# Neighbour maximum: word numbers added by the matrix engine, keys by five wide operations, and one joined tree over the ring slots

## What is computed

```python
def _L0_gnn_ref(X, adj):
    neg = jnp.finfo(X.dtype).min
    mask = adj != 0
    ...
        vals = jnp.max(jnp.where(mrows[:, :, None], X[None, :, :], neg), axis=1)
        has_nbr = jnp.any(mrows, axis=1)
        return (None, jnp.where(has_nbr[:, None], vals, jnp.zeros((), X.dtype)))
...
x = _layernorm(x + _L0_gnn_ref(x, adj), axis=-1)
```

## Time and profile before

| | |
|---|---|
| three plain runs, median | 4908.32 us (4907.93 to 4910.63) |
| the profiled execution, span | 5439.8 us |
| mean granted PE clock in it | 0.929 |
| PE busy | 4559.6 us (84%) |
| DVE busy | 4311.2 us (79%) |
| ACT busy | 2207.6 us (41%) |
| POOL busy | 1205.9 us (22%) |
| the neighbour maximum in the profiled execution | 0 to about 2240 us |
| in it, from 237 to 2143 us: PE, DVE, ACT, POOL busy | 1336, 1303, 900, 945 us of 1906 |

### The profile page before, as it was taken

How to read it: one execution, slowest core, us unless ns; L and a number is a source line. 1 busy time by engine, 2 the same in 40 slices (tenths; PEclk the granted TensorE clock), 3 DMA queues, 4 the chain that set the end, 5 groups by cost and what they waited for, 6 DMA issues and landing times. The chain is left out here.

```text
span 5439.8 us, 68010 instructions
## 1 busy us (share of the span) xinstructions
PE 4559.6 (84%) x22263; PEld 2172.7 (40%) x22263; DVE 4311.2 (79%) x7371; ACT 2207.6 (41%) x2430; POOL 1205.9 (22%) x1342
## 2 busy tenths in 40 slices
PE   4766776677667766579999999999999999999999
PEld 3333333333333333323443333454444445444444
DVE  6666676667666667788888888889999987999998
ACT  3444444444444444398888888410000001000000
POOL 5555445454444455200000000000000000000000
PEclk6888888888888889889999999999999999999999
DMA  7555555555555555233232332122222202212220
GB/s 272 195 187 184 192 197 185 187 182 194 186 179 188 193 169 166 95 130 122 105 126 111 113 127 105 64 102 83 75 84 79 81 9 99 102 70 98 76 96 14
DMA packets 181695, 709.72 MB, mean 130 GB/s; under 512 B 31168, under 2 KB 39872, under 8 KB 132224
## 3 DMA queue, kind: packets, MB, share of 16 engines
q1 hardware_dynamic: 110816, 566.01, 29.3%
q0 software_dynamic: 33760, 73.21, 4.2%
q10 hardware_dynamic: 36864, 67.13, 3.5%
HBM read 630.59 MB, written 79.82 MB: 131 GB/s over the span
## 5 line engine op out<-in xcount | busy, mean ns | idle before, releaser
L1750 PE MATMUL bank<-w,GX 128*128 128x512 f32 x4096 | 1768.4, 593 | 4.8 <-DVE w L1865 4.8
L1865 DVE SCALAR_TENSOR_TENSOR w<-q,E,m 128x512 f32<-128x512 f32 x2048 | 1472.1, 758 | 130.8 <-PE bank L1750 39.1
L356 POOL DMA_INDIRECT ring<-x_ext,idx x1051 | 1032.8, 983 | 1074.2 <-DVE X L619 316.8
L1750 PEld LDWEIGHTS bank<-w,GX 128*128 128x128 f32 x4096 | 777.7, 191 | 975.3 <-issue 975.2
L607 DVE TENSOR_TENSOR top<-top,sums 128x1024 f32<-128x1024 f32 x484 | 589.2, 1217 | 626.7 <-remote 364.8
L507 PE MATMUL sums<-lone,xs 128*128 128x512 fp8e4 x3000 | 838.3, 421 | 287.0 <-DVE top L607 214.9
L1200 PE MATMUL acc<-w,GX 128*128 128x512 f32 x2048 | 939.6, 605 | 65.8 <-DVE w L1458 62.6
L430 ACT ACTIVATE stage<-tp 128x1024 fp8e4<-128x1024 uint16 x512 | 523.7, 1025 | 1088.1 <-remote 598.3
L1458 DVE SCALAR_TENSOR_TENSOR w<-q,E,u 128x1024 f32<-128x1024 f32 x512 | 634.7, 1274 | 1.9 <-PE acc L1200 1.8
L507 PEld LDWEIGHTS sums<-lone,xs 128*128 128x128 bf16 x3000 | 291.5, 105 | 814.7 <-issue 607.4
L1200 PEld LDWEIGHTS acc<-w,GX 128*128 128x128 f32 x2048 | 371.9, 190 | 564.5 <-issue 413.5
(11 more groups left out here) (250 smaller groups left out, 2919.3 us busy)
## 6 DMA issues: line engine op xcount, KB each, us to landing
adjb<-in_adj SPq DMA_DIRECT2D x256, 1024.0 KB
m<-mask_t SPq DMA_DIRECT2D x128, 1024.0 KB, 4.8
mask_t<-stage ACTq DMA_DIRECT2D x256, 256.0 KB
den_m<-mask_t SPq DMA_DIRECT2D x64, 1024.0 KB, 6.9
keep_m<-mask_t SPq DMA_DIRECT2D x64, 1024.0 KB, 4.9
ring<-x_ext,idx POOLq DMA_INDIRECT x1051
z<-row_scores SPq DMA_DIRECT2D x30, 256.0 KB, 4.6
xt_rows<-XT SPq DMA_DIRECT2D x8, 512.0 KB, 4.7
```

The lines of the kernel that those rows point to most:

```text
L356: pool.indirect_dma_start(ring[:, s, :], None, x_ext, bass.IndirectOffsetOnAxis(ap=idx[:, k, s:s + 1], axis=0)).then_inc(done, 16)
L1750: last = nc.tensor.matmul(acc[b][:, :], GX[:, j, :], w[:, j % WR, :], start=(j == 0), stop=(j == T - 1))
L1865: nc.vector.scalar_tensor_tensor(out=w[:, j % WR, :], in0=q, scalar=E[:, j:j + 1], in1=m[:, b, j, :], op0=ALU.max, op1=ALU.mult).then_inc( ...
```

## The change

Three things change, all in `neighbour_max`.

1. **Word numbers by PE.** `one_row` (ones in one row) times `numbers` adds to every code in `tally` the number of its word, times 2^-7. It is one matmul of 512 columns in front of the counts of blocks 0 to 3 and one in front of those of blocks 4 to 7; the counts accumulate onto it. Half of the words, 256, are numbered; `half_no` tells the halves apart.
2. **Keys by five wide operations** in place of seven: the exponent of the code (line 702), the rest (720), the word's number put into the exponent's low bits (722), the minimum of that and `before`, which is now 2^20 times the earlier neighbours, so that it is zero in the group's first word (726), and a `max` for each half of the rest (730). ACT's `opens` is gone. `cnt_used` is now signalled by the minimum. The operations that follow the leftovers down are 16 wide instead of 8, and their results go into the first word's key of each group, which is unused: the list that is searched has 512 instead of 536 entries.
3. **One tree.** The tree over slots 0 to 11 stops at three slots, the other too, and a 384-column operation joins them. Slots 3 to 5 are free after the second level (`lower_free`), slots 0 to 2 only at the end (`rest_free`), and the gathers are put in that order.

```diff
@@ pool, tile
-                for part in range(3):
-                    follow(2 + part)
-                    gather(k, 2 * part, 2, gathered)
+                follow(2)
+                gather(k, HALF // 4, HALF // 4, gathered)
                 hold(pool, rest_free, t + 1)
+                follow(3)
+                gather(k, 0, HALF // 4, gathered)
                 gather(k, FIRST[1], SIZES[1], low_in)
@@ act
-                if 1 <= t <= T:
-                    act.wait_ge(counted, t)
-                    nc.scalar.activation(opens[:, :, 1:WPG], before, ACT.Relu, bias=top_bit[:, 0:1], scale=-TOP_BIT).then_inc(opens_made, 1)
@@ pe
             pe.wait_ge(again, 5)
+            pe.wait_ge(numbers_made, 1)
...
             def count(q, k, e):
 
+                if e % (T // TRB // HALVES) == 0:
+                    bank = slice(e * TRB, e * TRB + T // HALVES)
+                    nc.tensor.matmul(tally[:, bank, :].rearrange("p t c -> p (t c)"), one_row[:, :], numbers[:, :, :].rearrange("p t c -> p (t c)"),
+                                     start=True, stop=False, skip_group_check=True)
                 for g in range(e * TRB, (e + 1) * TRB):
-                    last = nc.tensor.matmul(tally[:, g, :], stage[:, q, g, k * P:(k + 1) * P], powers[:, :], start=True, stop=True)
+                    last = nc.tensor.matmul(tally[:, g, :], stage[:, q, g, k * P:(k + 1) * P], powers[:, :], start=False, stop=True, skip_group_check=True)
@@ dve, phase
-                    hold(dve, opens_made, s + 1)
-                    steps.did(nc.vector.tensor_tensor(out=bits(by_group(high)), in0=bits(code_ps), in1=bits(opens[:, :, :]), op=ALU.bitwise_and))
+                    steps.did(nc.vector.tensor_scalar(bits(keys[:, :, :]), bits(code_ps), EXPONENT, None, ALU.bitwise_and))
...
-                    nc.vector.tensor_tensor(out=by_group(x), in0=code_ps, in1=by_group(high), op=ALU.subtract).then_inc(cnt_used, 1)
-                if finishes:
-                    into(old, 0, 2).then_inc(lower_free, 1)
+                    steps.did(nc.vector.tensor_tensor(out=by_group(x), in0=code_ps, in1=keys[:, :, :], op=ALU.subtract))
+                    steps.settle()
+                    side.did(nc.vector.tensor_tensor(out=bits(not_opening), in0=bits(not_opening), in1=by_group(code_no[:, :])[:, :, 1:WPG], op=ALU.bitwise_or))
                 if extracts:
-                    hold(dve, cnt_used, s + 2)
-                    steps.do(nc.vector.tensor_scalar(bits(high), bits(x), EXPONENT, None, ALU.bitwise_and))
-                    steps.did(nc.vector.tensor_tensor(out=x, in0=x, in1=high, op=ALU.subtract))
+                    steps.settle()
+                    side.settle()
+                    nc.vector.tensor_tensor(out=not_opening, in0=not_opening, in1=before, op=ALU.min).then_inc(cnt_used, 1)
                 step(2)
                 if extracts:
-                    steps.settle()
-                    steps.did(nc.vector.tensor_tensor(out=bits(x), in0=bits(x), in1=code_no[:, :], op=ALU.bitwise_or))
-                    side.did(nc.vector.tensor_tensor(out=bits(high), in0=bits(high), in1=code_no[:, :], op=ALU.bitwise_or))
-                    steps.settle()
-                    steps.did(nc.vector.max(out=y, in_=x))
+                    for a in range(HALVES):
+                        steps.did(nc.vector.max(out=y[:, 8 * a:8 * a + 8], in_=x[:, a * HW:(a + 1) * HW]))
...
                     if finishes and d == 1:
-                        tree.did(larger(h, h, h + 1, 1))
+                        hold(dve, lower_free, old + 2)
+                        tree.did(larger(0, 0, h, h // 4))
                     if finishes and d == 2:
-                        tree.did(larger(h, h, h + 2, 1))
+                        tree.did(larger(0, 0, 1, 1))
...
                 if finishes:
-                    tree.settle()
-                    hold(dve, lower_free, old + 2)
-                    into(old, None, h).then_inc(rest_free, 1)
+                    into(old, 0, 2).then_inc(rest_free, 1)
```

More of the change, by code:

```diff
@@ L25 @@
 EXPONENT = 0x7F800000
-TOP_BIT = 2.0 ** WORD
-MORE = 8
+LEAST = 2.0
+HALVES = 2
+HW = NW // HALVES
+NUMBER = 2.0 ** -7
+BEFORE = 2.0 ** 20
+MORE = 8 * HALVES
 DEEP = 4
@@ L206, in neighbour_max @@
         codes = sb("codes", [P, NW], F32)
[L207 to L209 removed]
+        numbers = sb("numbers", [P, T // HALVES, COLS], BF16)
+        one_row = sb("one_row", [P, P], BF16)
+        half_no = sb("half_no", [P, HALVES, 8], I32)
+        keys = sb("keys", [P, T, WPG], F32)
         many = sb("many", [P, MORE], F32)
+        many_i = sb("many_i", [P, MORE], I32)
         many_no = sb("many_no", [P, MORE], I32)
[L212 removed]
+        many_high = sb("many_high", [P, T // MORE, MORE], F32)
         srt = sb("srt", [P, SRT], F32)
@@ L579, in _ @@
             steps.do(nc.vector.memset(ones[:, :], 1.0))
-            steps.do(nc.vector.memset(opens[:, :, :], TOP_BIT))
-            nc.vector.memset(top_bit[:, :], TOP_BIT).then_inc(opens_free, 1)
+            steps.did(nc.vector.memset(many_high[:, :, :], 0.0))
+            steps.do(nc.vector.memset(numbers[:, :, :], 0.0))
+            dve.wait_ge(words_numbered, 3)
+            steps.do(nc.vector.tensor_scalar(numbers[:, :, 0:WPG], code_no[:, 0:HW].rearrange("p (t w) -> p t w", w=WPG), NUMBER, None, ALU.mult))
+            nc.vector.tensor_copy(one_row[:, :], one_row_f).then_inc(numbers_made, 1)
             steps.do(nc.vector.memset(need[:, :, :], 0.0))
@@ L663, in phase @@
                 h = HALF
-                tops = tops and quad is not None and k == 0
+                turned = turned and quad is not None and k == 0
                 def bits(ap):
@@ L676, in phase @@
                 by_group = lambda ap: ap.rearrange("p (g w) -> p g w", w=WPG)
-                if tops:
+                not_opening = keys[:, :, 1:WPG]
+                listed = keys[:, :, :].rearrange("p g w -> p (g w)")
+                if turned:
                     merge(quad - 1)
@@ L722, in phase @@
                     steps.settle()
-                    steps.did(nc.vector.tensor_scalar(many_no[:, :], bits(y), NW - 1, None, ALU.bitwise_and))
+                    steps.did(nc.vector.tensor_scalar(many_i[:, :], y, 1.0 / NUMBER, None, ALU.mult))
                 if finishes:
@@ L728, in phase @@
                     steps.settle()
-                    steps.did(nc.vector.tensor_tensor(out=bits(y), in0=bits(y), in1=many_no[:, :], op=ALU.bitwise_xor))
+                    steps.did(nc.vector.scalar_tensor_tensor(out=many_no[:, :], in0=many_i[:, :], scalar=HW - 1, in1=half_no[:, :, :].rearrange("p a n -> p (a n)"),
+                                                             op0=ALU.bitwise_and, op1=ALU.bitwise_or))
                 if finishes:
@@ L746, in phase @@
                 if finishes:
-                    tree.settle()
-                    hold(dve, lower_free, old + 2)
-                    into(old, None, h).then_inc(rest_free, 1)
+                    into(old, 0, 2).then_inc(rest_free, 1)
                 if extracts:
-                    later = keys[:, NW:NW + (DEEP - 1) * MORE].rearrange("p (d n) -> p d n", n=MORE)
-                    steps.did(nc.vector.tensor_tensor(out=bits(later), in0=bits(many_high[:, :, :]), in1=many_no[:, :].unsqueeze(1).to_broadcast([P, DEEP - 1, MORE]), op=ALU.bitwise_or))
+                    later = keys[:, :, 0].rearrange("p (d n) -> p d n", n=MORE)
+                    steps.did(nc.vector.tensor_tensor(out=bits(later), in0=bits(many_high[:, :, :]), in1=many_no[:, :].unsqueeze(1).to_broadcast([P, T // MORE, MORE]), op=ALU.bitwise_or))
+                    hold(dve, cnt_used, s + 2)
                     side.settle()
                     steps.settle()
-                    steps.did(nc.vector.max(out=srt[:, 0:8], in_=keys[:, :]))
+                    steps.did(nc.vector.max(out=srt[:, 0:8], in_=listed))
                 step(5)
@@ L759, in phase @@
                         steps.settle()
-                        steps.did(nc.vector.match_replace(out=keys[:, :], in_to_replace=srt[:, 8 * r - 8:8 * r], in_values=keys[:, :], imm_value=0.0))
+                        steps.did(nc.vector.match_replace(out=listed, in_to_replace=srt[:, 8 * r - 8:8 * r], in_values=listed, imm_value=0.0))
                         steps.settle()
-                        steps.did(nc.vector.max(out=srt[:, 8 * r:8 * r + 8], in_=keys[:, :]))
+                        steps.did(nc.vector.max(out=srt[:, 8 * r:8 * r + 8], in_=listed))
                     step(5 + r)
```

35 lines of the change are left out of this document (16 added, 19 removed).

## The result

| kernel | median us (lowest to highest) | tile, us |
|---|---|---|
| before | 4908.12 (4901.22 to 4910.63) | 25.25 |
| after | 4977.68 (4974.04 to 4998.96) | 26.43 |

The changed kernel takes 1.0155 of the time before, with a 95% interval of 1.0134 to 1.0175: 70 us slower, where I had said 22, and above the range of 4895 to 4965. The direction held, the size didn't. The last column is the mean distance of a take from the one a tile later, over the same 56 tiles in each trace.

The account below looks back on a forecast made before the run. The first stage was taken as bound by PE and DVE alternating over the single `sums` buffer, with DVE setting four steps. 0.07 + 0.27 = +0.34 us a tile, +20 over 60 tiles, start +1.5, gave 4930 us; range 4895 to 4965.

Parts of the forecast that it names:

- The stops: Several engines standing at once in the profiled first stage: 9.1 us a tile, 510 us; plain runs have hardly any.
- The base of 24.8 us: Time of a tile before the change, from eight undisturbed steps (24.3 us) plus 0.5 for turning the maximum.
- The floor of 2.85 us and 1.7 us of free DVE work: Per step: PE and DVE alternate over single buffer `sums`; beside DVE's take of a summed pair, 1.7 us is free.
- DVE's busy time is what counts: Rival: plain runs are bound by DVE's work, 1.5 us a tile less, 4812 us (4876 with a third); chance 0.12.
- Take 0, mask at 0.68: Step ending at a tile's first take: mask against a constant costs 0.68 us, no gain; at 0.44, 0.24 less.
- To take 0 still 3.44: Sign in the trace after: undisturbed steps ending at a tile's first take stay at 3.44 us.
- GpSimd's queue: Gathers of slots 0 to 2 wait for `rest_free`; hidden if they land within 4 us.
- A wait behind the opening: Sign of being wrong: a wait for the gathers appears at the first tree operation.
- Takes 2 and 3: Key operations before them: the later `cnt_used` makes PE's count wait 0.46 us, PE late by 0.25; together +0.07 us.
- Take 5: Costly step holding the join: a 384-column operation replaces a 128-column one, +0.27 us a tile, bounds +0.25 to +0.40.
- The start: Kernel opening: more GpSimd and DVE steps for constants ahead of PE's first transposes at 7.33 us, about +1.5 us.
- The sum: Whole kernel: +0.34 us a tile, 60 tiles +20, opening +1.5, giving 4930 us; bounds 4899 to 4953.

Follow-up runs that it names:

- the second profile: The kernel before, unchanged, profiled once more: 4902.6 us, span 4904.9 us, 0.999 to 1.001 of before.
- the spread kernels: DVE's work spread over the steps, `need` with two tensors: new keys with old trees 4832.8 us (first try 4917.7), whole change 4841.5, before 4855.1.
- the two-tensor `need`: `need` computed by the operation form with a second tensor, same values: in after 4943.5 us (1.008), in before 4896.8 us (0.9986).
- The minimum first: After with the minimum that signals `cnt_used` moved ahead of the OR: 4958.3 us, 1.0115.
- the join alone: Before with only the joined tree and the new order of the gathers: 4966.1 us, 1.0131.
- the keys alone: After with before's two trees and order of gathers, so only PE's word numbers and the keys: 4925.0 us, 1.0051.
- the order alone: Before's own operations spread evenly over the steps, `need` with two tensors: 4855.1 us, against 4896.8 for before with only that `need`.

## Why the prediction was right or wrong

- **The stops aren't in plain runs: right.** The conclusion from the earlier trace rows and the median is borne out by the second profile. The base of 24.8 us was too low by 0.45: I read clean steps from single tiles and left out that `need` is held in some tiles, that PE is slow after some quads' ends, and that two tiles wait for gathers. That is in before and after, and so wasn't the error, but the place where the error would arise was in it.
- **The floor of 2.85 us and 1.7 us of free DVE work: right.** Takes are never regularly closer, steps 6 and 7 didn't move, and the spread kernels rest on it. "DVE's busy time is what counts" is refuted: 54.9 us less work, 67.4 us more span. The forecast of some 90 us less work was too high; 17.4 of the missing 35 are the longer `need`.
- **Take 0, mask at 0.68: right** (684 ns). **"To take 0 still 3.44": wrong** in a third of the tiles, for another reason.
- **GpSimd's queue, "hidden": this is the step that failed.** I costed the three gathers behind `rest_free` by when they land, and by this measure they are nearly hidden: DVE's 128 x 768 tree operations stood 17.3 us for gathers in all of their 128 times, against 14.8 in before. (A wait behind the opening, which I had named as a sign of being wrong, does appear, three times in after and twice in before.) I didn't follow what stands behind them on GpSimd: the memsets, moved into DVE's tail ahead of take 0. I had priced this at 0; the two-tensor `need` shows 34 us, some 24 in the holds and 10 in the slow PE behind them. It also was no rival of mine.
- **Takes 2 and 3: the mechanism was right, the size too small.** The predicted wait of the count for `keys` is there. I had 0.46 us for it, and it is 0.67; I had PE late by 0.25 and take 2 0.07 earlier, and in the tile shown PE is 0.30 late, and in the mean take 2 is 0.07 later. The sum is +0.25 a tile instead of +0.07 (upper bound 0.3). The minimum first gives back 19 us.
- **Take 5: +0.36 instead of +0.27** (bound 0.40). The join is +0.23 by the join alone, against the 0.27 costed. The rest is the work on 16 numbers: I had +0.03, and the shorter search took it back; the keys alone show +0.13.
- **The start: right.** PE's first transposes begin at 8.95 us instead of 7.33.
- **The sum.** Forecast +0.34 us a tile, measured +1.18: 0.50 for steps 0 and 1, 0.18 for steps 2 and 3, 0.09 for step 5, and 0.05 in step 4 (one step of 4.48 us makes up 0.03 of it; its cause is open) are missing (to rounding). Without the memset's part, 4943.5 would have lain in the range.

What stays open: why PE falls to the lower clock behind some idle stretches and not behind others of the same length. Nor does any run keep the join and put the memsets elsewhere, so what the moved wait costs is known from the holds, not from moving it back.

## What to carry to other kernels

Moving a wait in a queue moves everything that stands behind it, not only the transfers that it is about: follow each later instruction of that engine to the new place and ask whom it meets there. Where two engines take turns over a single buffer, work beside the turn is free up to a fixed amount per step, so count by step, and before making operations cheaper, move them from full steps into those with room: here the order alone gave 42 us, and the cheaper keys, a loss of 22 us in the old order, came with a further gain of 22 in an order made for them. A signal that another engine waits for goes out with the first instruction that can carry it.

## What the runs showed of the hardware

- A GpSimd memset of 1.16 us holds a DVE operation with one tensor, of three numbers a row, until it ends (1.38 and 1.57 us instead of 0.16), and not one with two tensors at the same place.
- After 2.74 us of idling PE ran part of the next 3.7 us at the lower level: mean granted clock 0.63, transposes 1.03 us instead of 0.61. In the second profile of before it stood 2.64 us before the same group and kept its clock (transposes 0.62 us). Of the 13 held tiles of after that aren't a quad's first, all with 2.24 to 2.26 us of idling before the sums, PE was slow in 6 (sums of 1.89 to 2.72 us) and not in 7 (1.46): the length of the idling doesn't decide it.
- One execution of the same kernel had some 510 us of stops on several engines, the second none: 5439.8 against 4904.9 us.
- Where gathers had to land before GpSimd went on, it stood 4.61 us after its memset, 3.2 of them for the last landing, which came 5.0 us after the start of the last gather (940.24 to 945.24).
